# The causal-window mask of a local-attention kernel on TensorE: eight half-array products or two full-array ones

## The reference

```python
q = l2norm(q) * qs                      # t / clip(norm(t), 1e-12)
k = l2norm(k) * ksc
q, k = rotary_xpos(q, k)
# local attention: windows of 128; keys of the window before and of the same one
sim = einsum('bhwid,bhwjd->bhwij', bq * 8.0, bk)
mask = (i < j) | (i > j + WINDOW) | (j == -1)
sim = where(mask, -max_float, sim)
attn = softmax(sim)
x = x + (attn @ bv) @ wo
```

## Time and profile before

| what | value |
| --- | --- |
| time, median of 3 runs (lowest to highest) | 2030.9 us (2029.85 to 2031.94) |
| the profiled execution: its own time | 2031.94 us |
| its span, first to last instruction | 2030.5 us |
| mean granted TensorE clock | 0.919 |
| busy: PE, PEld, DVE, ACT, POOL | 89%, 67%, 57%, 46%, 46% |
| GpSimd at the start: last memset of a_K (L322) ends, first L337 starts | 13.54 us, 14.28 us |
| issues of the zero rows on SyncE (L124) | 8, from 481.4 to 484.6 us |
| next issue of SyncE after them (L290) | 495.15 us |

### The profile page before, as it was taken

The page is one execution under the profiler, slowest core; times in us unless marked ns, Lnnn a source line. Parts: engine busy times, 40 slices in busy tenths (PEclk is TensorE's granted clock), DMA queues, the critical chain, the costliest instruction groups (busy, mean ns, idle before and its releaser), DMA issues. The chain is left out here.

```text
span 2030.5 us, 42787 instructions
## 1 busy us (share of the span) xinstructions
PE 1801.4 (89%) x14072; PEld 1357.6 (67%) x14072; DVE 1153.4 (57%) x2891; ACT 939.2 (46%) x1834; POOL 933.1 (46%) x919
## 2 busy tenths in 40 slices
PE   5999988889679999999979999599999999789887
PEld 4556655655357777777768888477777777577776
DVE  4556665656367776766523333776676666234343
ACT  2545555555335555455534444255545555333322
POOL 3345444554335565554423333355555555333433
PEclk7888888997779999999979999799999999799998
DMA  4333343333100000000121112100000000221221
GB/s 145 102 118 98 104 120 114 119 110 115 37 27 2 31 31 31 31 31 21 49 58 42 62 62 93 43 11 31 31 31 31 31 21 21 64 73 55 79 72 42
DMA packets 103736, 121.29 MB, mean 60 GB/s; under 512 B 23386, under 2 KB 75780, under 8 KB 103684
## 3 DMA queue, kind: packets, MB, share of 16 engines
q1 hardware_dynamic: 96772, 95.45, 15.7%
q0 software_dynamic: 6912, 25.17, 3.5%
HBM read 82.55 MB, written 37.77 MB: 59 GB/s over the span
## 5 line engine op out<-in xcount | busy, mean ns | idle before, releaser
L468 DVE TENSOR_REDUCE a_negm<-a_x 128x2 f32<-128x256 f32 (+3 forms) x256 | 202.8, 814 | 142.3 <-PE a_x L594 139.8
L864 POOL TENSOR_TENSOR work<-work 128x512 f32<-128x512 f32 x128 | 164.5, 1285 | 196.7 <-DVE work L1014 195.1
L430 ACT ACTIVATE a_PT<-a_c 128x384 f32<-128x384 f32 (+1 forms) x384 | 183.8, 522 | 140.8 <-PE a_c L633 87.7
L1539 DVE SCALAR_TENSOR_TENSOR m_hid<-m_a,mw_b,m_gate 128x512 f32<-128x512 f32 x96 | 71.9, 749 | 244.9 <-ACT m_gate L1477 220.8
L1032 DVE CUSTOM_DVE_ANT_0 l_x<-l_x,window 128x256 f32<-128x256 f32 (+1 forms) x512 | 183.9, 419 | 41.2 <-PE l_x L1129 40.9
L1063 PE MATMUL l_f<-w_hi,tails 128*128 128x512 f32 x384 | 170.6, 444 | 15.4 <-DVE work L1014 12.3
L1434 POOL TENSOR_TENSOR m_hid_lo<-m_hid,m_hid_hi 128x512 fp32r<-128x512 f32 x80 | 102.7, 1291 | 132.2 <-ACT m_hid_hi L1488 132.0
L941 ACT ACTIVATE l_PT<-l_c 128x512 f32<-128x512 f32 (+1 forms) x256 | 124.5, 538 | 74.4 <-PE l_c L1169 74.4
L1064 PE MATMUL l_f<-w_hi,tails 128*128 128x512 f32 x384 | 155.4, 405 | 0.0
L1065 PE MATMUL l_f<-w_lo,tails 128*128 128x512 f32 x384 | 154.2, 402 | 0.0
L878 POOL TENSOR_TENSOR l_PS<-l_PT 128x768 f32<-128x768 f32 x64 | 119.5, 1867 | 66.1 <-ACT l_PT L941 66.1
(11 more groups left out here) (239 smaller groups left out, 5140.8 us busy)
## 6 DMA issues: line engine op xcount, KB each, us to landing
a_Q<-qk_parts SPq DMA_DIRECT2D x192, 64.0 KB, 2.1
a_K<-qk_parts SPq DMA_DIRECT2D x192, 64.0 KB, 2.1
qk_parts<-a_qk_hi SPq DMA_DIRECT2D x32, 256.0 KB, 2.1
qk_parts<-a_qk_lo SPq DMA_DIRECT2D x32, 256.0 KB, 2.1
after_attn<-rows_out POOLq DMA_DIRECT2D x16, 512.0 KB, 5.3
xin<-after_attn SPq DMA_DIRECT2D x32, 256.0 KB, 3.1
m_xr<-after_attn SPq DMA_DIRECT2D x16, 512.0 KB, 4.1
xin<-in_L_attn_x SPq DMA_DIRECT2D x8, 512.0 KB, 3.5
```

The source lines that it names most:

```text
L430: nc.scalar.activation(PT[:, p // PG % 2, 2 * (p % PG) + hh, QOFF[t]:QOFF[t] + nq], SC[hh][:, 0:nq], ACT.Exp, scale=AD ** -0.5).then_inc(e ...
L468: dve.tensor_reduce(negm[:, q, 2 * p:2 * p + 2], MX[i % 2][:, :, 0:nk], AX.X, ALU.max, negate=True).then_inc(max_done, 1)
L864: pool.tensor_tensor(t1[:, par, w, :], t1[:, par, w, :], t2[:, par, w, :], ALU.add)\
```

## The change

Four edits:

- A new table window_t holds the mask with keys and queries exchanged, so that now the identity is the stationary operand and the mask moves: per unit two products of 512 columns with all 128 rows of the array, one for each head's bank, take the place of eight of 128 columns with 64 rows. Each of the two tells ScalarE that its bank is full. window and window_sw are still made; GpSimd has one memset and two selects more at the start.
- The clipping at L1010 takes its bound as an immediate number (tensor_scalar) and no longer as a second tile (tensor_tensor); the tile least, its memset and the wait for it go.
- The zero rows go out in 2 transfers of 256 numbers per sequence and no longer in 8 of 64. The tile is four times as wide.
- The count MADE follows the three more constants.

```diff
+        "window_t": sb("window_t", [P, 2, P], BF16),
...
+    pool.memset(k["window_t"][:, :, :], 0.0).then_inc(made, 1)
...
-    for m, n, sign in ((k["window"], 1, -1), (k["window"], 0, 1)):
+    for m, n, sign in ((k["window"], 1, -1), (k["window"], 0, 1), (k["window_t"], 0, 1), (k["window_t"], 1, -1)):
...
-            for c in range(0, DM, DM // 4):
-                sp.dma_start(a[:, 0, c:c + DM // 4], self.tile[:, :]).then_inc(self.out, 16)
+            sp.dma_start(a[:, 0, :], self.tile[:, :]).then_inc(self.out, 16)
...
-                            dve.tensor_tensor(ss[:, par, :], ss[:, par, :], least[:, :], ALU.max)\
+                            dve.tensor_scalar(ss[:, par, :], ss[:, par, :], 1e-24, None, ALU.max)\
                                 .then_inc(ss_done, 1)
...
-                        for n, table in enumerate((K["window"], K["window_sw"])):
-                            for blk in range(2):
-                                for hh in range(2):
-                                    rows, at = slice(FD * hh, FD * hh + FD), FD * (hh ^ n)
-                                    m = pe.matmul(SC[hh][:, :].rearrange("p (t b q) -> p t b q", t=2, b=2)
-                                                  [:, :, blk, at:at + FD], table[rows, 1 - blk, :],
-                                                  K["identb"][rows, FD * hh:FD * hh + FD].unsqueeze(1)
-                                                  .to_broadcast([FD, 2, FD]), start=False, stop=True,
-                                                  skip_group_check=True)
-                                    if n == 1 and blk == 1:
-                                        m.then_inc(sc_full, 1)
+                        mask = K["window_t"][:, :, :].rearrange("p b q -> p (b q)").unsqueeze(1).to_broadcast([P, 2, 2 * P])
+                        for hh in range(2):
+                            pe.matmul(SC[hh][:, :].rearrange("p (t q) -> p t q", t=2), K["identb"][:, :], mask,
+                                      start=False, stop=True, skip_group_check=True).then_inc(sc_full, 1)
```

More of the change, by code:

```diff
@@ L16 @@
 NEG = -1.0e30
-MADE = 12
+MADE = 15
 LN_EPS = 1e-5
@@ L90, in make_constants @@
     pool.memset(k["window"][:, :, :], 0.0).then_inc(made, 1)
+    pool.memset(k["window_t"][:, :, :], 0.0).then_inc(made, 1)
     pool.memset(k["window_sw"][:, :, :], 0.0).then_inc(made, 1)
-    pool.wait_ge(made, 5)
+    pool.wait_ge(made, 6)
     pool.affine_select(out=k["identb"][:, :], in_=k["identb"][:, :], compare_op=ALU.not_equal, fill=1.0, base=0,
                        pattern=[[-1, P]], channel_multiplier=1).then_inc(made, 1)
-    for m, n, sign in ((k["window"], 1, -1), (k["window"], 0, 1)):
+    for m, n, sign in ((k["window"], 1, -1), (k["window"], 0, 1), (k["window_t"], 0, 1), (k["window_t"], 1, -1)):
         pool.affine_select(out=m[:, n, :], in_=m[:, n, :], compare_op=ALU.is_ge, fill=NEG, base=0,
@@ L113, in __init__ @@
     def __init__(self, nc, ctx, rows):
-        self.rows, self.tile = rows, ctx.enter_context(nc.sbuf_tensor("zero_row", [NB, DM // 4], F32))
+        self.rows, self.tile = rows, ctx.enter_context(nc.sbuf_tensor("zero_row", [NB, DM], F32))
         self.made, self.out = ctx.enter_context(nc.semaphore("zero_set")), ctx.enter_context(nc.semaphore("zero_out"))
@@ L122, in store @@
         for a in self.rows:
-            for c in range(0, DM, DM // 4):
-                sp.dma_start(a[:, 0, c:c + DM // 4], self.tile[:, :]).then_inc(self.out, 16)
+            sp.dma_start(a[:, 0, :], self.tile[:, :]).then_inc(self.out, 16)
     def done(self, sp):
-        sp.wait_ge(self.out, 64 * len(self.rows))
+        sp.wait_ge(self.out, 16 * len(self.rows))
 def first_attention(nc, K, scr, w, xin, rows_out, zeros, ahead, x, w_qkv, b_qkv, w_out, b_out, dst):
@@ L743, in local_attention @@
         sq = work[:, 2 * n_t + n_qk:2 * n_t + n_qk + 2 * INNER].rearrange("p (w n) -> p w n", w=2)
-        ss, inv, least = sb("ss", [P, 2, 2 * FH]), sb("inv", [P, 2, 2 * FH]), sb("least", [P, 2 * FH])
+        ss, inv = sb("ss", [P, 2, 2 * FH]), sb("inv", [P, 2, 2 * FH])
         QH, QL = sb("QH", [P, FH // 2, S + P], F32R), sb("QL", [P, FH // 2, S + P], F32R)
@@ L770, in local_attention @@
         YB = [OB, SB]
-        small, least_set = sem("small"), sem("least_set")
+        small = sem("small")
         q_set, negm_set, pick_zero, pick_set = sem("q_set"), sem("negm_set"), sem("pick_zero"), sem("pick_set")
@@ L966, in rotary_factors @@
                 def rotary_factors():
-                    dve.memset(least[:, :], 1e-24).then_inc(least_set, 1)
                     dve.wait_ge(rots_in, 96)
@@ L978, in rotary_factors @@
                     dve.wait_ge(rots_done, 6)
-                    dve.wait_ge(least_set, 1)
                     dve.memset(negm[:, :, :, :], 0.0).then_inc(negm_set, 1)
```

## The result

The changed kernel takes 2047.56 us (median of 4 runs, 2045.24 to 2049.13), the kernel before beside it 2030.57 us (median of 4). The ratio is 1.0090, with 95% from 1.0079 to 1.0102. The change costs 17 us, about 0.9%, where I had forecast 10.

The account below looks back on a forecast made before the run. TensorE was taken to set the pace, busy 54.79 of 56.74 us an iteration. Terms 9.8 + 3.4 + 2.6 - 2.5 - 1.4 - 2 + 0.1 = +10.0 us gave 2041 us, range 2034 to 2049.

Parts of the forecast that it names:

- Each mask in front of a projection: Five units per local_attention iteration: the block grows from 0.79 to 0.93 us, +0.14 each, 70 times, +9.8 us.
- rival C: Masks are cheaper because their first weight load is hidden: +0.09 us each, +5 us in all, 2036 us; chance 0.12.
- I take half of the exposed 0.11: First new mask product: its 16-bit weight load shows 0.05 us, half of what a float32 load shows.
- st:7: Last mask unit, before half-array f_sm:1: gets two switches, f_t:2 loses its wait; +0.24 us, x 14 = +3.4 us.
- St:5 and st:6 are hidden: Mask units before pv:2: the 0.3 to 0.4 us each adds on TensorE is covered by waiting for exponentials, costing nothing.
- piece (2): At st:5 the exponentials start at 746.4 in place of 746.53: -0.1 us, x 14 = -1.4 us.
- if st:5 or st:6 now delays pv:2: Stated sign that the forecast is wrong: these masks hold up pv:2; without cover they would cost 10 us.
- The last sequences: Last sequence of each layer, overlapping no next one: head 0's later mask delays units, +1.3 us a layer, +2.6 us.
- the new one for a plain one-input instruction: Clipping at L1010: the tensor_scalar takes 0.1 to 0.17 us and does not wait for GpSimd.
- Rival A: The clipping still waits for GpSimd, pieces (1) to (3) vanish, f_qk:7's wait swallows 1.5 us: +14.4, 2045 us; chance 0.2.
- pieces (1): f_qk:7's wait for VectorE's L1014 shrinks: 0.27 us an iteration in layer one, about 0.1 in layer two, -2.5 us.
- (3): First sequence's projections before each loop: about half of eight 0.5 us stalls on VectorE go, -2 us.

Follow-up runs that it names:

- Runs 5: The changed kernel with the eight old half-array mask products at st:5 only; 2047.22 us, ratio 1.0081.
- 12: The changed kernel with clipping by tensor_reduce, unused tiles where ss and least stood, and the old mask at st:5 only; 2036.51 us, ratio 1.0027.
- run 7: The kernel before with clipping by tensor_reduce over pairs, all other tiles kept in their places; 2024.49 us, ratio 0.9976.
- run 2: The kernel before with only the clipping changed to tensor_scalar and the tile least gone; 2030.88 us, ratio 1.0008.
- runs 4: The kernel before with clipping by tensor_reduce over pairs into its own tile, other tiles moved; 2026.84 us, ratio 0.9985.
- run 6: The changed kernel with an unused tile of 64 bytes per partition where least stood; 2042.40 us, ratio 1.0060.
- run 1: The kernel before with the new mask products and their table alone, old clipping and zero rows; 2042.54 us, ratio 1.0064.
- the two further profiles: The changed kernel profiled again twice, unaltered; 2047.80 and 2047.39 us, ratios 1.0084 and 1.0081.

## Why the prediction was right in sign and what failed in it

- **Each mask in front of a projection**: forecast +0.14, measured +0.09 to +0.10 by the rows and 0.085 by the shift of the iteration. The term of 9.8 us was mis-sized; it is 70 x 0.085 = 6.0 us, as rival C had it. The failed part is "I take half of the exposed 0.11". Nothing of the 16-bit load shows. The switch (0.09) and the pace (0.227) were right.
- **st:7**: forecast +3.4 us, measured 14 x 0.21 = 2.9. Right.
- **st:5 and st:6**: the step that failed is "St:5 and st:6 are hidden". St:6 is; st:5 costs 0.30 us an iteration, 14 x 0.30 = 4.2 us in all. I had read the earlier trace rows as pv:2 waiting for the exponentials of st:5, and had not followed what stands behind st:5 on TensorE itself: sv:1, whose sums reach pv:2 by way of ScalarE's logarithm and VectorE's zn:1. Runs 5 and 12 show it: undoing the mask at st:5 alone gives 0.22 to 0.29 us in layer one, and 0.30. The -1.4 us of piece (2), the earlier exponentials of st:5, falls with the same reading: run 7 has them 0.26 us earlier and gains nothing at pv:2. I had named the sign, "if st:5 or st:6 now delays pv:2", and the price without cover as 10 us for both.
- **The last sequences**: forecast +2.6 us. Between the last products of out of the two last sequences lie 43.9 and 44.0 us in layers one and two, in the mean of the five profiles with the old mask, and 45.0 and 44.5 in the mean of six with the new one, so 1.5 us more; but single profiles of one kind differ by up to 2 us, so this term is not measured well.
- **The clipping**: the failed step is "the new one for a plain one-input instruction". Run 2 measures 737 ns in the mean. L1572 misled me: it takes its scalars from tiles and never runs beside a busy GpSimd in the trace (nor do the four alike of first_attention, L518, which I had overlooked when I called it the only one), so its pace of one element per step did not tell whether a tensor_scalar with an immediate waits. Rival A had the mechanism: pieces (1) to (3) are absent, and f_qk:7's wait, which stays, swallows part of the mask. It had 1.5 us for that; measured are 7 x 0.20 in layer one and 7 x 0.10 in layer two, 2.1 us.
- **Pieces (1) and (3)** exist, as runs 4 and 7 show with a clipping that really does not wait: 0.23 us an iteration in layer one and 1.9 us in its first sequence's projections.
- **Not foreseen at all**: the places of the tiles (run 6: 0.43 us in each of 7 iterations, about 3 us), and the lost handovers to GpSimd (0.91 us each, two in each of the two further profiles, whose second local_attention is 2.7 and 3.5 us longer than in the first, part of it in the first sequence). The second is my reading of why the timed runs lie 4 us above the first profile, in which none was lost. It is argued and not shown: for it, first_attention takes 543.9 to 544.2 us in all three profiles; against taking it for sure, the profiled execution of run 6 lies 4 us above that kernel's median too and has no lost handover, but 549.1 us of first_attention.

The sum as measured: 6.0 + 2.9 + 4.2 - 2.1 + 1.5 = 12.5 us for the mask, with which run 1 (ratio 1.0064, 13 us) and run 6 (1.0060) agree (the two local_attentions of run 6 take 504.8 and 503.3 us, 13.0 more than before). With 3 for the places and about 3 for the handovers it is 18 to 19, against 17 us timed. The forecast of 10 had the masks in front of projections too dear, by 3.8 us, and four other things too cheap, by 4.2 + 1.4 (st:5), about 2 (the first projections), 3 and 3. That 2047.6 us lies inside the range of 2034 to 2049 is therefore luck in part: the forecast's own case was wrong on the clipping and on st:5, A was right on the clipping and C on the masks, neither had st:5, and 6 of the 17 us come from two causes that nobody had named. What stays open is why the place of a tile changes the pace of the products that read from SBUF, and which tile it is: the runs show only that 64 bytes of shift do it. That the kernel before has no long iteration needs no other form of the clipping: there it comes 0.32 us before the handover. Whether a two-input clipping at the handover would lose it too was not tried.

## What to carry to other kernels

Before an added cost is called hidden, follow everything that stands behind it: its consumer on the other engine, and also the next instructions on its own engine and whom they feed. When eight half-array products become two full-array ones, count the columns that each part of the array still has to take, and the switches on both sides, not instructions: here 48 fewer instructions an iteration cost 0.7 us. And when an allocation goes away with an edit, keep its place with an unused tile until the edit itself is measured.

## What the runs showed of the hardware

- A tensor_scalar of 128x16 float32 with an immediate bound waits for GpSimd's running instruction like a tensor_tensor (174 to 1336 ns); a tensor_reduce over twice the data does not (186 ns in the mean). Whether the tensor_scalar slips in between two instructions of GpSimd that follow without a gap is decided within about 0.02 us, and decides 0.91 us of an iteration.
- A shift of tiles by 64 bytes changes the distance of float32 products of 256 columns from 0.1134 to 0.1198 us, at the same granted clock of 1.00; shifts of 512 and 1280 bytes did not.
- The first 16-bit 128x128 weight load behind a change from half-array to full-array products showed nothing (0.21 us to the first mask, 0.227 to the second), where a float32 one shows 0.11.
